# Loading, normalising and aggregating the two graphs of the first group separately, in a graph-network and mixture-of-experts kernel

## The reference

```python
x = x + gnn(layernorm(x), adj)     # adj: 32 x 256 x 256
x = x + ffn(layernorm(x))          # 8 experts, the 2 best per token

def gnn(xn, adj):
    agg = epsilon * xn + adj @ xn          # per graph, 256 x 256 by 256 x 128
    h = agg @ W1 + b1                      # 128 -> 512
    h = silu(rmsnorm(h) * rms_weight)
    return h @ W2 + b2                     # 512 -> 128
```

## Time and profile before

| | |
|---|---|
| time, median of 3 runs | 412.56 us (412.33 to 413.8) |
| profiled execution, its own time | 411.64 us |
| its span, from the first to the last instruction | 409.8 us |
| mean granted clock of TensorE in it | 0.998 |
| PE busy | 383.1 us (93%) |
| POOL, DVE, ACT busy | 314.5, 300.9 and 278.9 us |

### The profile page before, as it was taken

The page is one execution under the profiler, slowest core; times in us unless marked ns, Lnnn a source line. Parts: engine busy times, 40 slices in busy tenths (PEclk is TensorE's granted clock), DMA queues, the critical chain, the costliest instruction groups (busy, mean ns, idle before and its releaser), DMA issues. The chain is left out here.

```text
span 409.8 us, 11327 instructions
## 1 busy us (share of the span) xinstructions
PE 383.1 (93%) x2598; PEld 324.8 (79%) x2598; DVE 300.9 (73%) x1290; ACT 278.9 (68%) x653; POOL 314.5 (77%) x440
## 2 busy tenths in 40 slices
PE   2899999999999999999789999988989999999994
PEld 1467777767777777777669999978878999999993
DVE  5687789999999999998865744665555666765562
ACT  1377777797777898779777657766766876555540
POOL 1233368877787898988888889999866677999984
PEclk9999999999999999999999999999999999999999
DMA  7979983444433442221256225555555555531111
GB/s 236 277 227 341 322 253 125 131 144 148 147 87 104 155 144 79 80 66 54 68 161 193 70 87 148 147 142 159 147 142 143 155 156 160 150 86 40 38 38 38
DMA packets 43472, 57.25 MB, mean 140 GB/s; under 512 B 6224, under 2 KB 36176, under 8 KB 42768
## 3 DMA queue, kind: packets, MB, share of 16 engines
q1 hardware_dynamic: 35200, 36.74, 32.0%
q0 software_dynamic: 6096, 18.52, 12.9%
q10 hardware_dynamic: 2112, 1.27, 1.1%
HBM read 41.80 MB, written 22.31 MB: 156 GB/s over the span
## 5 line engine op out<-in xcount | busy, mean ns | idle before, releaser
L568 POOL DMA_INDIRECT out<-result,rows_in x92 | 90.5, 983 | 28.3 <-DVE result L1569 16.2
L818 PE MATMUL banks<-w_sb,hidden_e 128*128 (+1 forms) x736 | 101.3, 279 | 0.2 <-issue 0.2
L818 PEld LDWEIGHTS banks<-w_sb,hidden_e 128*128 128x128 f32 x736 | 91.0, 192 | 1.2 <-issue 0.6
L958 ACT ACTIVATE hidden_e<-banks 128x512 f32<-128x512 f32 x92 | 55.0, 597 | 45.6 <-PE banks L801 44.1
L511 POOL DMA_INDIRECT rows_dram<-rows_out,row_of x64 | 65.3, 1021 | 13.5 <-issue 10.6
L645 PE MATMUL banks<-gw_sb,agg 128*128 128x512 f32 x128 | 65.2, 595 | 0.9 <-DVE gw_sb L1009 0.9
L669 PE MATMUL banks<-hidden_t,gw_sb 128*128 128x256 f32 x256 | 62.3, 386 | 1.7 <-ACT hidden_t L881 1.7
L524 POOL MEMSET space<- 128x620 f32 x100 | 63.0, 630 | 0.1
L669 PEld LDWEIGHTS banks<-hidden_t,gw_sb 128*128 128x128 f32 x256 | 46.4, 190 | 16.1 <-ACT hidden_t L881 7.3
L1104 DVE TENSOR_TENSOR hidden<-banks,rms_bc 128x512 f32<-128x512 f32 x64 | 43.9, 687 | 15.3 <-ACT hidden L866 15.1
L1555 DVE SCALAR_TENSOR_TENSOR acc<-banks,rows_in,acc 128x128 f32<-128x128 f32 x72 | 25.3, 351 | 33.2 <-PE banks L818 25.0
(11 more groups left out here) (148 smaller groups left out, 740.5 us busy)
## 6 DMA issues: line engine op xcount, KB each, us to landing
rows_in<-rows_dram SPq DMA_DIRECT2D x92, 132.5 KB, 2.3
adj<-adj_t SPq DMA_DIRECT2D x16, 512.0 KB, 4.4
x_tok<-x SPq DMA_DIRECT2D x16, 256.0 KB, 5.4
x_d<-x_t SPq DMA_DIRECT2D x16, 256.0 KB, 4.7
rows_dram<-idle_in POOLq DMA_DIRECT2D x1, 3710.0 KB, 13.8
rows_dram<-idle_in SPq DMA_DIRECT2D x28, 132.5 KB
out<-result,rows_in POOLq DMA_INDIRECT x92
w_sb<-w SPq DMA_DIRECT2D x1, 1024.0 KB, 8.1
```

Source lines behind the costliest of these rows:

```text
L568: nc.gpsimd.indirect_dma_start(out=out, out_offset=bass.IndirectOffsetOnAxis(ap=rows_in[:, i % RING][:, IDX_AT:IDX_AT + 1].bitcast(U32), a ...
L818: last = pe.matmul(y_ps(i)[:, w], hidden_e[:, i % 4, w * HCE + c], w2_sb[:, bass.ds(at + c * D, D)], start=(c == 0 and i >= EARLY), stop=( ...
L958: nc.scalar.activation(hidden_e[:, i % 4], h_ps(i), ACT.Gelu).then_inc(gelu_done, 1)
```

## The change

Of group 0 alone, SP loads `x_tok` and `adj` in two halves each, one graph's half at a time, in the order x, adj, x, adj; the first halves have semaphores of their own (`x_first`, `adj_first`), the second halves signal `x_in[0]` and `adj_in[0]`. DVE computes the statistics, adds epsilon and normalises graph by graph (`first_stats`, `first_epsilon`, `first_rows`), GpSimd takes the power in two instructions of two columns, and PE waits for each graph's adjacency separately. `prep_ident` now stands between the statistics of the two graphs. All later groups are as before.

```diff
--- before.py
+++ after.py
@@ -267,6 +267,12 @@
         x_in = [sem(f"x_in{k}") for k in range(XR)]
         x_d_in = [sem(f"x_d_in{k}") for k in range(XD)]
         adj_in = [sem(f"adj_in{k}") for k in range(AR)]
+        x_first = sem("x_first")
+        adj_first = sem("adj_first")
+        head_link = sem("head_link")
+        stats1_first = sem("stats1_first")
+        rstd1_first = sem("rstd1_first")
+        adj_first_ready = sem("adj_first_ready")
         fixed_in_sbuf = sem("fixed_in_sbuf")
         gw1_in = sem("gw1_in")
         gb1_in = sem("gb1_in")
@@ -407,6 +413,13 @@
                     sp.wait_ge(xn1_ready, g - XR + 1)
                 if g == 2:
                     sp.wait_ge(adj_in[1], 16)
+                if g == 0:
+
+                    sp.dma_start(x_tok[:, 0, 0:2], x_view[0][:, 0:2]).then_inc(x_first, 16)
+                    sp.dma_start(adj[:, 0, 0:2], adj_view[0][:, 0:2]).then_inc(adj_first, 16)
+                    sp.dma_start(x_tok[:, 0, 2:4], x_view[0][:, 2:4]).then_inc(x_in[0], 16)
+                    sp.dma_start(adj[:, 0, 2:4], adj_view[0][:, 2:4]).then_inc(adj_in[0], 16)
+                    continue
                 sp.dma_start(x_tok[:, g % XR], x_view[g]).then_inc(x_in[g % XR], 16)
                 if g >= AR:
                     sp.wait_ge(agg_done, g - AR + 1)
@@ -459,6 +472,14 @@
             pool.wait_ge(pool_consts, 1)
 
             def scale1(g):
+                if g == 0:
+                    pool.wait_ge(stats1_first, 1)
+                    nc.gpsimd.tensor_tensor(rstd1[:, 0, 0:2], var1[:, 0, 0:2], minus_half[:, 0:2], ALU.pow
+                                            ).then_inc(rstd1_first, 1)
+                    pool.wait_ge(stats1_ready, 1)
+                    nc.gpsimd.tensor_tensor(rstd1[:, 0, 2:4], var1[:, 0, 2:4], minus_half[:, 2:4], ALU.pow
+                                            ).then_inc(rstd1_ready, 1)
+                    return
                 pool.wait_ge(stats1_ready, g + 1)
                 if g >= 2:
                     pool.wait_ge(xn1_ready, g - 1)
@@ -619,9 +640,10 @@
             def aggregate(g):
                 if g == 0:
                     pe.wait_ge(xn1_half, 1)
+                    pe.wait_ge(adj_first_ready, 1)
                 else:
                     pe.wait_ge(xn1_ready, g + 1)
-                pe.wait_ge(adj_ready, g + 1)
+                    pe.wait_ge(adj_ready, g + 1)
                 if g >= 1:
                     pe.wait_ge(agg_copied, g)
                 if g >= 3:
@@ -629,6 +651,7 @@
                 for b in range(2):
                     if g == 0 and b == 1:
                         pe.wait_ge(xn1_ready, 1)
+                        pe.wait_ge(adj_ready, 1)
                     for c in range(2):
                         last = pe.matmul(agg_ps[:, b * NODES:(b + 1) * NODES], xn1[:, g % 2, 2 * b + c],
                                          adj[:, g % AR, 2 * b + c], start=(c == 0), stop=(c == 1))
@@ -1077,6 +1100,48 @@
                     nc.vector.tensor_scalar(var1[:, g % 2], mv1[:, g % 2, :, 1], LN_EPS, None, ALU.add
                                             ).then_inc(stats1_ready, 1)
 
+            def first_stats(half):
+
+                tiles = slice(2 * half, 2 * half + 2)
+                if half:
+                    dve.wait_ge(x_in[0], 16)
+                else:
+                    dve.wait_ge(x_first, 16)
+                nc.vector.bn_stats(bn1[:, 2 * half], x_tok[:, 0, 2 * half])
+                nc.vector.bn_stats(bn1[:, 2 * half + 1], x_tok[:, 0, 2 * half + 1]).then_inc(
+                    bn1_done if half else head_link, 1)
+                dve.wait_ge(bn1_done if half else head_link, 1)
+                nc.vector.bn_aggr(mv1[:, 0, 2 * half], bn1[:, 2 * half])
+                nc.vector.bn_aggr(mv1[:, 0, 2 * half + 1], bn1[:, 2 * half + 1]).then_inc(
+                    aggr1_done if half else head_link, 1)
+                if half:
+                    dve.wait_ge(aggr1_done, 1)
+                else:
+                    dve.wait_ge(head_link, 2)
+                nc.vector.tensor_scalar(var1[:, 0, tiles], mv1[:, 0, tiles, 1], LN_EPS, None, ALU.add
+                                        ).then_inc(stats1_ready if half else stats1_first, 1)
+
+            def first_epsilon(half):
+                if half:
+                    dve.wait_ge(adj_in[0], 16)
+                else:
+                    dve.wait_ge(eps_ready, 1)
+                    dve.wait_ge(adj_first, 16)
+                for c in range(2):
+                    block = adj[:, 0, 2 * half + c, c * P:(c + 1) * P]
+                    last = nc.vector.tensor_tensor(block, block, eps_ident[:], ALU.add)
+                last.then_inc(adj_ready if half else adj_first_ready, 1)
+
+            def first_rows(half):
+                if half:
+                    dve.wait_ge(rstd1_ready, 1)
+                else:
+                    dve.wait_ge(rstd1_first, 1)
+                for t in (2 * half, 2 * half + 1):
+                    last = nc.vector.tensor_scalar(xn1[:, 0, t], x_tok[:, 0, t], mv1[:, 0, t, 0:1], rstd1[:, 0, t:t + 1],
+                                                   ALU.subtract, ALU.mult)
+                last.then_inc(xn1_ready if half else xn1_half, 1)
+
             def normalise1(g):
                 dve.wait_ge(rstd1_ready, g + 1)
                 if g >= 2:
@@ -1084,13 +1149,9 @@
                 for t in range(TPG):
                     last = nc.vector.tensor_scalar(xn1[:, g % 2, t], x_tok[:, g % XR, t], mv1[:, g % 2, t, 0:1],
                                                    rstd1[:, g % 2, t:t + 1], ALU.subtract, ALU.mult)
-                    if g == 0 and t == 1:
-                        last.then_inc(xn1_half, 1)
                 last.then_inc(xn1_ready, 1)
 
             def add_epsilon(g):
-                if g == 0:
-                    dve.wait_ge(eps_ready, 1)
                 dve.wait_ge(adj_in[g % AR], 16 * (g // AR + 1))
                 for c in range(2):
                     blocks = adj[:, g % AR].rearrange("p (b c) n -> p b c n", c=2)[:, :, c, c * P:(c + 1) * P]
@@ -1306,7 +1367,15 @@
                 nc.vector.tensor_tensor(left_row[:], whole[0:1, :], region[0:1, 0:NC], ALU.add).then_inc(ends_ready, 1)
 
             prep()
-            for s in range(STEPS):
+            first_stats(0)
+            prep_ident()
+            first_stats(1)
+            first_epsilon(0)
+            first_rows(0)
+            first_epsilon(1)
+            first_rows(1)
+            mix_gw1()
+            for s in range(1, STEPS):
                 g0, g2, g4, g5 = (group_at(s, lag) for lag in (0, 2, 4, 5))
                 if s == 3:
                     prep_rank()
@@ -1348,8 +1417,6 @@
                     route(g5, 5)
                 if g0 is not None:
                     stats1(g0, 2)
-                if s == 0:
-                    prep_ident()
                 if s == 1:
                     fold_gw1()
                 if turned:
@@ -1395,8 +1462,6 @@
                     table(0, 8)
                 if g0 is not None:
                     normalise1(g0)
-                if s == 0:
-                    mix_gw1()
                 if g5 is not None:
                     share_rows(g5, 0)
                 if after_known:
```

## The result

The changed kernel takes 413.78 us (median of 19 runs, 412.83 to 418.03), the kernel before 412.56 us (19 runs beside them, 411.08 to 413.94). The ratio is 1.0044, with a 95% interval of 1.0031 to 1.0057: slower by 1.2 us between the medians, where I had forecast 0.6 us faster. The ratio is above that of the medians (1.0030), since the changed kernel's runs reach further up, to 418.03 us. The profiled execution has a span of 411.9 us (409.8 before) and a mean granted clock of 0.993 (0.998 before).

A forecast was written before the change was run, and what follows sets the result against it. PE was taken as a gapless train from about 22 us, bound by its start. Loads 0, DVE's start -0.58, PE's clock 0, fold 0, later loads 0 gave -0.58 us: 412.56 to 412.0 us, range 411.0 to 413.6.

The forecast's parts named there:

- The train without gaps: PE from about 22 us on: busy without idle time, so the end moves with when this train starts.
- the rival in which each pays for a start of its own: Group 0's half loads don't overlap: x's second half at 8.25 us, PE 2.16 us late, total 414.7 us; chance 0.05.
- DVE's other input to `fold_gw1`: Bias load `gb1` on ACT, issued 1.27 us later, lands at 10.26; DVE ready at 12.40, adding 0 to the sum.
- the cover: DVE's reserve at `fold_gw1` before PE's result at 12.52 us: 0.1 us left of 1.9, used up but holding.
- the gain of 0.58: PE's first matmul at 7.51 us instead of 8.09, carried through `sum_weights` to `fold_gw1` at 12.52 instead of 13.10.
- Neither takes the gain back: SP's adjacency loads for groups 1 and 2 keep 1.5 and 2.8 us of slack, so later loads add 0.
- PE's clock 0: Term for PE's rise from 1.2 to 2.4 GHz near `sum_weights`: it adds 0 us to the sum.
- I assume that this change moves with the start of the work: PE's rise to 2.4 GHz comes earlier with its first matmul, so `sum_weights` ends 0.58 us earlier.
- The one on the other side of zero: x's second half lands late, from 6.1 us on, delaying all behind it on DVE and ACT: 412.7 to 414; chance 0.14.
- The gain is absorbed: x's second half lands at about 6.1 us, or `gb1` takes 0.6 us longer: total 412.6 us; chance 0.22.
- The clock does not move with the start: PE's clock rise stays within L710; about half of the 0.58 us is lost in `sum_weights`: 412.3 us; chance 0.07.

The follow-up runs named there:

- e8: The kernel before, nothing cut, with ACT issuing its three loads only when DVE's statistics of group 0 are done; ratio 1.0061 [1.0037, 1.0085].
- e1: The changed kernel run again without any edit; ratio 1.0025 [1.0001, 1.0049] against the kernel before.
- e9: The changed kernel with two more matmuls behind `sum_weights`, into a bank nobody reads, to keep PE busy; ratio 1.0018 [0.9998, 1.0038].
- e2: The changed kernel with ACT issuing its loads when the first half of x has landed, not the second; ratio 1.0010 [0.9981, 1.0038].
- e5: The changed kernel with bias and norm weights read from the rows of `gw1`, no common row; one run, 413.65 us beside 413.37 for the kernel before.
- e10: Computation graph by graph as in e4, x loaded whole, only the adjacency in halves; ratio 1.0013 [0.9988, 1.0038].
- e11: The same kernel as e4, word for word, measured again; ratio 0.9995 [0.9969, 1.0021].
- e4: The changed kernel with group 0's x and adjacency loaded whole, only the computation graph by graph; ratio 1.0011 [0.9985, 1.0037].
- e13: The kernel before, run again without any edit for its trace; one run, 412.12 us beside 412.26.
- e6: The changed kernel with the halves loaded in the order x, x, adjacency, adjacency; ratio 1.0059 [1.0028, 1.0090].
- e12: e8 with bias and norm weights read from the rows of `gw1`, no common row; one run, 415.10 us beside 415.14 for the kernel before.

## Why the prediction was wrong

**What held.** The landings of the halves (forecast 3.5 and 5.33 us for x, 6.6 for the second adjacency half; measured 3.4, 5.5 and 6.3), DVE's second statistics (5.56 forecast, 5.55 measured), its first rows (6.81 and 6.86) and PE's start (7.51 and 7.55). DVE waited less for epsilon (4.37 instead of 5.12), which changed nothing, as x's second half was awaited anyway. PE had no gap between the graphs. The train without gaps carried the shift to the second stage, as the earlier trace rows had suggested. The halves do overlap, so the rival in which each pays for a start of its own did not come true: x's second half landed at 5.5 us and not at 8.25. The prediction had set beside it the 2.0 us for each load of the Trainium skill, "DMA: Bandwidth & Descriptors", section on the anatomy of one DMA, with x's second half at 8.0 us; the trace does not agree. That section is about loads issued from GpSimd, and these are issued from SyncE.

**The step that failed** is that of DVE's other input to `fold_gw1`: "Moved, it lands at 10.26". I moved the load by 1.27 us and kept its duration of 4.5 us. It was issued 0.15 us later still (5.91 instead of 5.76), took 5.4 us and landed at 11.3. The prediction had itself said that the cover was used up to 0.1 us and that every further delay costs one for one, and then put the most likely case on the side where it holds. With the bias at 11.39 instead of 10.30, `fold_gw1` is at 13.39 instead of 12.5: the gain of 0.58 is gone and 0.29 us lost. e8 shows that late loads of ACT, alone, are enough for a loss of this size.

**Two other steps failed with it.** "Neither takes the gain back" was said of the later loads: group 1's adjacency had 1.5 us of slack in the sum and landed 2.2 us later (3.4 in e1, where it set the time). And the term "PE's clock 0" is wrong in two ways. The clock fell: PE, done earlier and waiting longer, stood still for 2.40 us, and the granted clock was 0.50 from 13.95 to 17.3 us. This made the first widening 0.95 us longer, which holds up the second aggregation by 0.24, and the second aggregation itself 0.53 us longer. The third aggregation was forecast at 21.01 us and started at 22.64: of these 1.63 us the late bias makes 0.87, seen at `fold_gw1`, and the slow clock 0.76. e9 takes 0.6 us back by keeping PE busy.

And the rise of the clock did not move with the start. "I assume that this change moves with the start of the work" carries the whole gain of 0.58 us from PE's first matmul to `sum_weights`. In e2, e5, e10 and e11 the bias is in time and PE starts 0.3 to 0.6 us earlier than in the kernel before, and yet `sum_weights` ends at 12.8 to 13.1 us, as before (13.06), because its clock rises at 12.4 to 13.4. Of the kernels with the bias in time only e4, with the rise at 11.11, passes a gain on (third aggregation at 20.80). So even with the bias in time most of these executions would not have had the forecast gain.

**The rivals.** The one on the other side of zero was right in sign and wrong in place: it had x's second half late. x came as forecast; what waits for it on ACT was late. That the measured 413.78 us lies in its 412.7 to 414 is chance. "The gain is absorbed" named `gb1` taking 0.6 us longer, the true place, but ended at zero, because it counted neither the adjacency nor the clock. "The clock does not move with the start", with a chance of 0.07, is what most traces with the bias in time show; it deserved more. The range, 411.0 to 413.6, missed the 413.78 by 0.2 us.

**What stays open.** Why reading one row from all partitions is slow in the late kernels and not in the early ones, why ACT's first load at 4.19 us (e13) is early enough and at 4.87 (e6) is not, and what sets the moment at which the clock rises, is not shown. The second stage's own spread, over 2 us, is not explained by anything that I changed.

No version beats the kernel before: e2, e4, e9, e10 and e11 cannot be told from it within their intervals.

## What to carry to other kernels

When one load's semaphore is moved to a later half, list everything that waits for it, other engines' DMA issues included, and give each moved load a duration from both sides; a load that starts at another moment meets other traffic. Where a sum uses the last tenth of a reserve, the likeliest case is not the one in which it holds. To start PE earlier is worth nothing while another input of the next step stays, and it can cost: PE then idles in the middle, with its clock to lose. A gain at PE's first instruction has to be followed through the rise of the clock before it is counted.

## What the runs showed of the hardware

The three loads of 256 KB that ACT issues (2 KB packets, 84 ns in the median in every run) have a mean of 86 to 99 ns when the first is issued from 3.4 to 4.2 us and 128 to 166 ns when it is issued from 4.87 us on. In the changed kernel 25 of the 384 packets take over 600 ns, before none does, and from 6 to 10 us the core moves 184 instead of 354 GB/s with its DMA engines nearly as busy (0.91 against 1.04). Two of the three read one 2 KB row for all 128 partitions; in order of their start the middle third of the packets, where most of the bias is, takes 234 ns in the mean against 90 before. Without the common row the mean of all is 107 to 119 ns, with another load beside them 105.

The granted clock fell to 0.50 within a pause of PE of 2.40 us (changed kernel) and, in e1, within one of 1.80 us that followed one of 1.12; with the pauses of 0.88 and 0.51 us in the kernel before, and of 0.88 and 1.56 us in e12, it stayed at 1.00. In two executions of the changed kernel, with PE's first matmul at 7.55 and 7.56 us, it rose at 10.50 and at 12.68 us.
